# Scores by key in a gated cross-attention block: four 32-row passes on strips of the array against one 128-row matmul a head, with operands stacked by way of HBM

## What is computed

```python
x = x + jnp.tanh(g_xattn[0]) * _L0_xattn_ref(_layernorm(x, axis=-1), ctx_768, Wq, bq, Wk, bk, Wv, bv, Wo, bo)
x = x + jnp.tanh(g_ffn[0]) * _L0_ffn_ref(_layernorm(x, axis=-1), weight_q, weight_scale, bias)

# _L0_xattn_ref
q = _split_heads(x @ Wq + bq)
k = _split_heads(y @ Wk + bk)
v = _split_heads(y @ Wv + bv)
scale = 1.0 / math.sqrt(D_HEAD)
scores = jnp.einsum('bhqd,bhkd->bhqk', q, k) * scale
weights = jax.nn.softmax(scores, axis=-1)
out = jnp.einsum('bhqk,bhkd->bhqd', weights, v)

# _L0_ffn_ref, one row of x2d
x_scale = jnp.maximum(jnp.max(jnp.abs(x2d), axis=-1, keepdims=True), EPS) / 127.0
x_q = jnp.clip(jnp.round(x2d / x_scale), -128, 127).astype(jnp.int8)
acc = jax.lax.dot_general(x_q, weight_q, (((1,), (1,)), ((), ())), preferred_element_type=jnp.int32)
out = acc.astype(jnp.float32) * x_scale * weight_scale[None, :] + bias
```

## Time and profile before

| | before |
|---|---|
| device time, three runs | 809.88, 810.26, 813.82 us (median 810.26) |
| span of the profiled execution | 808.9 us (the page gives no time of its own beside the span) |
| TensorE, VectorE, ScalarE, GpSimd busy | 98%, 72%, 69%, 65% |
| granted TensorE clock, mean | 0.998 |
| DMA | 79.68 MB, mean 99 GB/s; the queue of SP takes 30.3% of 16 engines |
| a step in mid kernel | 48.1 us a step on average from 80.3 to 754.3 us |

### The profile page before, as it was taken

The page is one execution under the profiler, slowest core; times in us unless marked ns, Lnnn a source line. Parts: engine busy times, 40 slices in busy tenths (PEclk is TensorE's granted clock), DMA queues, the critical chain, the costliest instruction groups (busy, mean ns, idle before and its releaser), DMA issues.

```text
span 808.9 us, 17171 instructions
## 1 busy us (share of the span) xinstructions
PE 794.3 (98%) x6658; PEld 523.0 (65%) x6658; DVE 582.8 (72%) x916; ACT 556.0 (69%) x845; POOL 523.9 (65%) x518
## 2 busy tenths in 40 slices
PE   9899999999999999999999999999999999999996
PEld 6665666666666766667667666667667666666563
DVE  4877788676767768678686767758568676767778
ACT  5676577675776667676676776667676675776685
POOL 4626484775947568494684947668485674855688
PEclk9999999999999999999999999999999999999999
DMA  8632604152151423314242161422413141111112
GB/s 288 222 77 82 201 28 131 67 161 69 39 170 53 137 79 74 123 53 140 76 138 70 43 188 50 122 80 79 136 54 118 66 104 55 54 49 56 53 53 105
DMA packets 39631, 79.68 MB, mean 99 GB/s; under 512 B 6912, under 2 KB 8320, under 8 KB 37504
## 3 DMA queue, kind: packets, MB, share of 16 engines
q1 hardware_dynamic: 38976, 77.75, 30.3%
q10 hardware_dynamic: 576, 0.85, 0.3%
HBM read 61.78 MB, written 16.81 MB: 97 GB/s over the span
## 4 chain that ended last, share of the span: by engine, by line
PE 89%; DVE 6%; issue 2%; ACT 2%; POOL 0%; DVEq 0%; ACTq 0%; POOLq 0%
PE bank_b L340 29%; PE bank_a L340 19%; PE scores L395 8%; PE sum_ps L426 7%; PE scores L412 7%; PE pv_ps L430 6%; PE bank_a L474 5%; PE scores L417 2%; PE bank_b L474 2%; DVE row_max L1095 2%; PE bank_a L449 1%; PE sum_ps L403 1%; DVE q_lo L1106 1%; PE pv_ps L674 1%; PE scores L370 1%
## 5 line engine op out<-in xcount | busy, mean ns | idle before, releaser
L1095 DVE TENSOR_REDUCE row_max<-scores 128x16 f32<-128x1920 f32 x64 | 138.0, 2157 | 125.8 <-PE scores L395 125.8
L1436 POOL TENSOR_TENSOR o_lo<-on,o_hi 128x512 fp32r<-128x512 f32 x48 | 68.5, 1427 | 130.6 <-ACT o_hi L791 130.6
L773 ACT ACTIVATE probs<-scores 120x2048 f32<-120x2048 f32 x64 | 120.5, 1882 | 39.8 <-PE scores L417 39.7
L1444 POOL TENSOR_TENSOR x<-x,gbias_r 128x512 f32<-128x512 f32 x64 | 82.5, 1292 | 26.2 <-ACT cen L797 25.2
L395 PEld LDWEIGHTS scores<-k_sb,q_sb 32*128 32x128 f32 x2048 | 62.9, 186 | 53.0 <-issue 52.3
L1402 POOL TENSOR_TENSOR xt<-xt,rstd_b 128x512 f32<-128x512 f32 x60 | 91.4, 1569 | 2.4 <-ACT rstd_b L1029 2.1
L1432 POOL TENSOR_TENSOR x<-x,gbo_r 128x512 f32<-128x512 f32 x64 | 83.7, 1320 | 2.1 <-DMA x<-in_x 2.0
L791 ACT ACTIVATE o_hi<-on 128x512 fp32r<-128x512 f32 x48 | 30.3, 632 | 72.9 <-DVE on L1116 72.8
L340 PE MATMUL bank_b<-xt_hi,wq_hi 128*128 128x512 f32 x188 | 79.4, 422 | 0.5 <-DVE xt_lo L1085 0.5
L1449 POOL TENSOR_TENSOR x<-x,u_sb 128x512 f32<-128x512 f32 x56 | 73.6, 1314 | 8.0 <-DVE u_sb L1184 7.9
L395 PE MATMUL scores<-k_sb,q_sb 32*128 32x120 f32 x2048 | 74.7, 282 | 1.3 <-issue 0.9
(11 more groups left out here) (222 smaller groups left out, 1974.9 us busy)
## 6 DMA issues: line engine op xcount, KB each, us to landing
xt<-in_x_t SPq DMA_DIRECT2D x16, 1024.0 KB, 6.4
x<-in_x SPq DMA_DIRECT2D x64, 256.0 KB, 2.8
out_x<-x SPq DMA_DIRECT2D x61, 256.0 KB, 2.0
x_in<-in_x SPq DMA_DIRECT2D x60, 256.0 KB, 3.5
rstd_b<-rstd_rows SPq DMA_DIRECT2D x14, 256.0 KB, 5.0
ctx_sb<-in_ctx_t SPq DMA_DIRECT2D x8, 360.0 KB, 4.9
probs<-in_wq SPq DMA_DIRECT2D x4, 256.0 KB, 3.6
x<-in_wo SPq DMA_DIRECT2D x1, 1024.0 KB, 8.9
```

Of the source, the lines that this page charges most:

```text
L773: act.activation(probs[0:KEYS], scores[0:KEYS], ACT.Exp, scale=SCALE).then_inc(p_ready, 1)
L1095: dve.tensor_reduce(row_max[:].rearrange("p (t r) j -> p r t j", r=ROWG)[:, :, :, j], scores[:, :, 0:QT * KEYS].rearrange("p r (t k) -> p ...
L1436: pool.tensor_tensor(o_lo[i % 2][j], on[:], o_hi[i % 2][j].bitcast(F32), ALU.subtract).then_inc(o_split, 1)
L1444: pool.tensor_tensor(x1_of(m)[:, t], x1_of(m)[:, t], gbias_r[:], ALU.add).then_inc(x1b_ready, 1)
```

## The change

All of `scores_by_key` becomes one matmul of 128 rows a head, four a chunk, with nothing accumulated. Rows 0 to 95 of the stationary `k_stack` are k high, k high, k low, those of the moving `q_stack` q high, q low, q high. Rows 96 to 127 of `k_stack` hold, once and for all, minus a choice of the head's two rows, and those of `q_stack` the turned maxima of all heads, high and low. [...] `copy_max` now writes four copies of the maxima to strip 3 of `q_stack[0]` in one instruction of 32 x 2048, and `spread_max` copies that strip by DMA to `q_stack[1]`. The keys are split a pair of batches at a time (`split_high_k`, `split_low_k`). `q_parts` is one buffer: `split_high(n, j)` waits until the chunk before is stored.

```diff
+            def store_q(n, j):
+                sp.wait_ge(q_split, nth(n, DT, j))
+                if n > 0:
+                    sp.wait_ge(q_stacked[j % 2], 48 * nth(n - 1, 2, j // 2))
+                sp.dma_start(q_rows[j].rearrange("h p s -> p h s"), q_parts[:].bitcast(F32)).then_inc(q_stored, 16)
+
+            def stack_q(n, j):
+                sp.wait_ge(q_stored, 16 * nth(n, DT, j))
+                if n > 0 or j >= 2:
+                    sp.wait_ge(s_done, nth(n, DT, j) - 2)
+                for block, part in enumerate((0, 1, 0)):
+                    load(q_stacked[j % 2], q_stack[j % 2][STRIPS[block]].bitcast(F32),
+                         q_rows[j, part].rearrange("(r d) s -> d r s", d=DH))
...
+            def stack_k(n, h):
+                sp.wait_ge(k_stored[h], 16 * nth(n // 2, 2, 1))
+                if n > 0:
+                    sp.wait_ge(s_done, nth(n - 1, DT, 2 * h + 1))
+                heads = slice(h * HEADS // 2, (h + 1) * HEADS // 2)
+                for block, part in enumerate((0, 0, 1)):
+                    rows_of = k_rows[n // 2 % 2, part, 2 * h:2 * h + 2].rearrange("j (r d) k -> d (j r) k", d=DH)
+                    load(k_stacked[h], k_stack[STRIPS[block], heads].bitcast(F32), rows_of[:, :, keys_of(n)])
+
+            def spread_max(n):
+                sp.wait_ge(max_copied, nth(n, 1))
+                if n > 0:
+                    sp.wait_ge(s_done, nth(n - 1, DT, 3))
+                top = q_stack[0][STRIPS[3], 0:1].bitcast(F32)
+                load(max_spread, q_stack[1][STRIPS[3]].bitcast(F32), top.broadcast_to([DH, ROWG, S]))
...
+                spread_max(i)
                 if is_batch(e):
                     store(e, 0)
                 if is_batch(f):
                     load_x(f, 2)
+                if i > 0:
+                    store_q(i, 2)
+                stack_q(i, 2)
...
             def scores_by_key(i, j):
-                pe.wait_ge(qk_split, nth(i, 2 * DT, 2 * j + 1))
-                q, k = (q_hi[j % 2], q_lo[j % 2]), (k_hi[j % 2], k_lo[j % 2])
-                for p, (a, b) in enumerate(((0, 0), (0, 1), (1, 0))):
-                    for r in range(ROWG):
-                        pe.matmul(scores[0:KEYS, r], k[a][STRIPS[r]], q[b][STRIPS[r]], start=p == 0, stop=False)
+                pe.wait_ge(q_stacked[j % 2], 48 * nth(i, 2, j // 2))
+                pe.wait_ge(k_stacked[j // 2], 48 * nth(i, 1))
                 if j == 0:
                     pe.wait_ge(max_copied, nth(i, 1))
+                if j == 1:
+                    pe.wait_ge(max_spread, 16 * nth(i, 1))
                 for r in range(ROWG):
-                    rows = slice(r * DH, r * DH + PAIR)
-                    ins = pe.matmul(scores[0:KEYS, r], pick[rows, j:j + 1].broadcast_to([PAIR, KEYS]), max_t[rows],
-                                    start=False, stop=True)
+                    ins = pe.matmul(scores[0:KEYS, r], k_stack[:, j * ROWG + r], q_stack[j % 2][:, r], start=True, stop=True)
                 ins.then_inc(s_done, 1)
...
+            def split_high(n, j):
+                act.wait_ge(q_ready, nth(n, DT, j))
+                if n > 0 or j > 0:
+                    act.wait_ge(q_stored, 16 * (nth(n, DT, j) - 1))
+                act.activation(q_parts[:, 0], q_of(n, j), ACT.Copy).then_inc(q_hi_done, 1)
...
             def copy_max(n, bank):
                 act.wait_ge(max_turned, nth(n, 1))
-                act.activation(max_t[:], bank[:], ACT.Copy).then_inc(max_copied, 1)
+                act.activation(q_stack[0][STRIPS[3]], bank[STRIPS[3]].unsqueeze(1).broadcast_to([DH, ROWG, S]),
+                               ACT.Copy).then_inc(max_copied, 1)
```

More of the change, by code:

```diff
@@ L182, in key_tiles, with q_of, k_parts_of @@
             return n // 2, 2 * (n % 2), 2 * (n % 2) + 1
+        def q_of(n, j):
+            return u_tail[:, j - 1] if n == 0 and j >= 2 else q_sb[j % 2][:]
+        def k_parts_of(pair, j):
+            if pair > 0:
+                return k_parts[:]
+            tile = o_lo0[:, j] if j < DT - 1 else o_lo_end[:]
+            return tile[:, 0:2 * KEYS2].rearrange("p (h k) -> p h k", h=2)
         def x1_of(n):
@@ L194, in gated_layer @@
         zt_last = [xt[:, 2 + t // 2, (t % 2) * (D // 2):(t % 2 + 1) * (D // 2)].bitcast(BF16) for t in range(QT)]
-        u_own = [q_sb[:, t] for t in range(QT)]
+        u_own = [q_sb[0][:], q_sb[1][:], x_in[:, 0], x_in[:, 1]]
         u_last = [u_tail[:, c] for c in range(CT)] + [rstd_b[:]]
@@ L273, in _ @@
             load(rest_landed, ident_b[:], consts_bf16)
+            for j in range(DT):
+                store_k(0, j)
+            store_q(0, 0)
+            stack_k(0, 0)
+            stack_k(0, 1)
+            stack_q(0, 0)
             load_x(2, 0)
@@ L276, in _ @@
             load_ctx(1)
+            store_q(0, 1)
+            stack_q(0, 1)
+            store_q(0, 2)
             load_x(2, 2)
@@ L294, in step @@
                     load_residual(i, 0)
+                store_q(i, 3)
                 if is_batch(f):
@@ L315, in step @@
                     load_x(f + 1, 1)
+                if is_batch(b):
+                    stack_q(b, 1)
                 load_residual(i, 3)
@@ L855, in step @@
                     quant_round(e, 3)
+                split_high(i, 3)
                 if keys_next:
@@ L925, in step @@
                     high_x(n, 3)
+                if is_batch(b):
+                    split_high(b, 2)
                 if keys_next and i > 0:
@@ L1019, in _ @@
             split_high(0, 0)
+            for j in range(DT):
+                split_high_k(0, j)
             for c in range(1, CT):
@@ L1038, in _ @@
             high_x(1, 3)
+            split_high(0, 2)
             high_ctx(1)
@@ L1358, in _ @@
             scale_q0(2, bank_a)
+            split_low(0, 0)
+            for j in range(DT):
+                split_low_k(0, j)
             maxima(0, 1)
-            split_low(0, 0)
             x_statistics(1, 3)
@@ L1365, in _ @@
             low_max(0)
+            split_low(0, 1)
             low_x(1, 0)
```

141 lines of the change are left out of this document (88 added, 53 removed).

## The result

| | before | changed |
|---|---|---|
| median of the runs, same chip | 812.04 us (4) | 893.23 us (4, 886.27 to 899.64) |
| ratio | | 1.097, interval 1.093 to 1.100 |
| span of the profiled execution | 808.9 us | 893.0 us |
| granted TensorE clock, mean | 0.998 | 0.952 |
| DMA | 79.68 MB | 187.40 MB |

Of the four runs of the changed kernel the slowest, 899.64 us, counts as a slow one and is left out of the ratio, so the ratio is not quite 893.23 over 812.04.

A forecast was written before the change was run, and what follows sets the result against it. TensorE, busy 98% of the span, was taken as the bound. Span 808.9 + start 34.9 + mid kernel 6 - last steps 4 = 846, with medians 1.4 above the span: 847 us; 8-in-10 range 818 to 888.

The forecast's parts named there:

- Switches saved: Each scores_by_key call on TensorE: whole matmuls avoid mode changes between array and strips, 0.42 us a call, 26 us saved.
- Start: Before step 0 and in steps 0 and 1: late operands through SP's queue and a lower clock add 34.9 us.
- Mid kernel: Steps 2 to 12: stalls of 2.25 us against 1.68 saved, a loss of 0.57 a step, +6 us in all.
- The chain through SP: Mid-kernel steps: the late chunk 2 query store delays ScalarE, then TensorE; stall 2.6 us even, 1.3 odd, mean 1.95.
- Turn: Turn of each step: TensorE waits for the larger copy of the maxima, 0.3 us a step (bounds 0.1 and 0.8).
- From step 13 on: Steps 13 to 15: no xt to load, so 1.3 us saved in each, -4 us in all.
- Narrow loads: Rival: loads into 32 partitions move at half rate, adding 2.5 us a step in eleven steps; 880 us, chance 0.27.
- Hidden stores: Rival: SP's queue runs at its best rate, eleven steps give -12 us, the start 4 less; 825 us, chance 0.12.
- The saved switches: Rival, faster: small transfers do not wait for large ones ahead, so stalls stay below 26 us; 800 us, chance 0.06.
- No gain from whole matmuls: Rival: each whole matmul pays for its weights or new bank, so 26 us come back; 873 us, chance 0.04.

The follow-up runs named there:

- whole_yield: Kernel before with whole matmuls only (scores wrong, nothing through HBM), GpSimd waiting for VectorE's low-part subtraction of queries before its last-chunk biases: 789.29 us, ratio 0.971.
- steps_early: Changed kernel with the spread of the maxima and the chunk 2 query store issued ahead of spread rstd and xt in every step: 842.39 us, ratio 1.039.
- the best kernel: Changed kernel with early issues in steps and start, more start-up moves on SP and ScalarE, and the maxima copied in halves: 818.31 us, ratio 1.009.
- spread_early_only: Changed kernel with only the spread of the maxima issued ahead of rstd and xt in every step, chunk 2 store unmoved: 896.21 us, ratio 1.100.

## Why the prediction was right and wrong

- **Switches saved** (26 us): right. 0.42 a call in place, 23.6 us in `whole_yield`. But my sign for it, TensorE's busy time down by some 20 us, did not come: it rose by 11.2, since matmuls at the low clock count as busy for longer.
- **Start** (34.9 us): right in place and order, 42.4 measured. Ahead of chunk 1 of step 0 TensorE was idle for 15.9 us (forecast 14.5), ahead of chunk 2 for 7.8 (6.1), ahead of chunk 1 of step 1 for 5.5 (5.9). The clock I priced at 1.5 us at the gap and a share of 2.5 behind it; 18.7 us of low clock were measured in steps 0 and 1, part of them inside the idle stretches. Of the 37.1 us added there, 30.4 are idle time and 6.7 longer busy time, in spite of the switches saved: the clock was priced too low here too.
- **Mid kernel** (+0.57 a step): the failed step, 3.74 measured. The chain through SP was right, and the stall itself near (2.56 for 1.95): the odd steps, to which I gave 1.3, stalled for 2.3 us on average, the even ones for 2.7. Two terms were missing. The low clock behind the stalls is 1.68 a step, 18.5 us in eleven steps, more than half of the miss of 35 there; the sum had it at nothing. I had written of the clock at the start and did not ask the same of the stalls of a step. And `spread_max(i)` I priced in step 1 only, though it stands behind xt in every step; waits for it are 0.33 a step, out of 0.70 lost in chunk 0, and that chunk is 0.45 shorter in `steps_early`.
- **Turn** (0.3): right, 0.23 of wait, 0.36 with what else chunk 3 lost.
- **From step 13 on** (-4): +0.5. A load of stacked queries (0.8 us) and the copy (1.4) are waited for in the last step, where there is little else to do.
- **Rivals.** Narrow loads: the rate was as said (200 against 354), but the stall did not grow by the 2.5 us a step that this rival has; 880 us is nearer to 893 than the forecast by accident, since more of the extra time came from the clock. Hidden stores is what `steps_early` made true in mid kernel by order alone, and there the steps gain 0.82, not the 1.1 forecast. The price of that rival has a slip: at 402 GB/s the sum gives T + 12.9 and T + 12.0, not 13.2 and 12.2, about 2 us less in all. The saved switches did not win: the 256 KB of the spread maxima, issued directly behind xt, landed 9.1 us later, 0.9 behind xt. No gain from whole matmuls is refuted by `whole_yield`.
- The range was too tight upwards: its bounds were bounds of waits, and in mid kernel none of them carried a price for the clock.

## What to carry to other kernels

A stall on TensorE can cost its length and then the clock behind it, here behind 2.2 to 3.4 us in nine of eleven steps: price both in mid kernel too, not only at the start. An operand that newly goes through a shared in-order queue is late by what stands ahead of it there: moving two issues ahead of 1 MB gave 50 of 81 lost us back, while the store alone gave 8 by the ratios (11 by the medians) and the spread none. And a gain taken from the engine that bounds must pay the start-up first, where in these runs no engine's work hid the round trip through HBM: the best kernel still paid 17 us there.

## What the runs showed of the hardware beyond that

- A VectorE subtraction of two SBUF operands (0.7 to 1.2 us) can be kept out for the whole of a gapless row of GpSimd instructions: 7.4 us, ten times in one execution, none in the trace with one wait on GpSimd. "SBUF — State Buffer" of the Trainium skill (two separate sides) has a port pair, shared by the two engines, held for a full instruction. If that pair is the cause, which no run here shows, it was lost for six instructions running.
- The clock did not answer to the length of one wait: 2.60 and 2.65 us left it up in two steps, while steps with 2.2 us of idle time lost 1.6. In `spread_early_only` a step with 2.8 us kept it, and one with 2.1 lost it.
